# A graph layer's matrix product: batches taken in pairs, adjacency steps reordered, and spare matrix work while the degrees are computed

## What is computed

```python
# x: (8, 2048, 128)   adj: (2048, 2048)   W: (128, 128), all float32
h      = relu(layernorm(x))              # over the last axis
A      = relu((adj + adj.T) / 2)
D      = A.sum(1);  d = D ** -0.5
L      = eye - d[:, None] * A * d[None, :]
out    = x + relu(einsum('nm,bmo->bno', L, einsum('bnf,fo->bno', h, W)))
```

## Time and profile before

| | us |
|---|---|
| median of 3 timed executions (448.17 to 450.79) | 448.46 |
| the profiled execution's own time | 449.94 |
| its span, first to last instruction | 448.00 |
| busy: TensorE / weight loads | 398.3 / 208.6 |
| busy: DVE / ACT / POOL | 186.3 / 118.2 / 177.9 |
| mean granted TensorE clock, share of full | 0.954 |

### The profile page before, as it was taken

How to read it: one execution, slowest core, us unless ns; L and a number is a source line. 1 busy time by engine, 2 the same in 40 slices (tenths; PEclk the granted TensorE clock), 3 DMA queues, 4 the chain that set the end, 5 groups by cost and what they waited for, 6 DMA issues and landing times.

```text
span 448.0 us, 5765 instructions
## 1 busy us (share of the span) xinstructions
PE 398.3 (89%) x2179; PEld 208.6 (47%) x2179; DVE 186.3 (42%) x507; ACT 118.2 (26%) x247; POOL 177.9 (40%) x287
## 2 busy tenths in 40 slices
PE   3628672999399999999999999999999999999994
PEld 3628560444145444544454445554444444444442
DVE  3686756968368664764577012111111111111111
ACT  1464766543234433342344011000000000000000
POOL 0198900599965874877185001221211121111111
PEclk9888695899889999999999999999999999999998
DMA  8999970432104200230032003331111111111101
GB/s 280 356 359 384 382 193 23 118 104 85 47 1 119 72 0 1 76 113 1 1 94 72 23 1 94 95 94 48 47 48 47 48 47 48 47 49 47 47 25 47
DMA packets 59307, 42.38 MB, mean 95 GB/s; under 512 B 1808, under 2 KB 51088, under 8 KB 59280
## 3 DMA queue, kind: packets, MB, share of 16 engines
q1 hardware_dynamic: 59280, 42.02, 30.2%
HBM read 33.62 MB, written 8.39 MB: 94 GB/s over the span
## 4 chain that ended last, share of the span: by engine, by line
issue 41%; PE 26%; POOL 17%; SPq 5%; DVE 4%; ACT 4%; DMA 2%; POOLq 0%; ACTq 0%
PE ps L553 7%; PE ps L554 7%; PE ps L555 7%; POOL sums L275 6%; POOL hbuf L257 3%; SPq L179 3%; DMA S<-in_adj_dram 2%; ACT S L307 2%; POOL lnt L241 2%; SPq L193 2%; PE ps L514 2%; PE ps L528 2%; POOL dsv L266 2%; POOL xn L257 1%; DVE S L383 1%
## 5 line engine op out<-in xcount | busy, mean ns | idle before, releaser
L554 PE MATMUL ps<-S,hbuf 128*128 128x512 f16 x512 | 196.1, 383 | 0.0
L553 PE MATMUL ps<-S,hbuf 128*128 128x512 f16 x496 | 188.8, 381 | 7.1 <-DVE S L398 7.1
L555 PE MATMUL ps<-S,hbuf 128*128 128x512 f16 x496 | 188.7, 381 | 0.0
L275 POOL TENSOR_TENSOR sums<-res,sums 128x512 f32<-128x512 f32 x32 | 42.6, 1335 | 194.8 <-DVE res L411 192.9
L553 PEld LDWEIGHTS ps<-S,hbuf 128*128 128x128 f16 x496 | 48.7, 98 | 62.8 <-DVE S L398 7.6
L333 ACT ACTIVATE g<-ps 128x512 f16<-128x512 f32 x32 | 19.1, 597 | 221.1 <-PE ps L555 185.0
L554 PEld LDWEIGHTS ps<-S,hbuf 128*128 128x128 f16 x512 | 50.5, 99 | 57.6 <-issue 1.9
L555 PEld LDWEIGHTS ps<-S,hbuf 128*128 128x128 f16 x496 | 48.7, 98 | 59.0 <-issue 0.8
L403 DVE SCALAR_TENSOR_TENSOR g<-ps,g 128x512 f16<-128x512 f32 x32 | 21.9, 685 | 112.7 <-ACT g L333 112.6
L411 DVE SCALAR_TENSOR_TENSOR res<-ps,dsv 128x512 f32<-128x512 f32 x32 | 22.1, 692 | 88.2 <-PE ps L569 88.2
L327 ACT ACTIVATE S<-S,dneg 128x512 f16<-128x512 f32 x62 | 43.7, 716 | 37.4 <-DVE S L398 35.4
(11 more groups left out here) (67 smaller groups left out, 263.2 us busy)
## 6 DMA issues: line engine op xcount, KB each, us to landing
S<-in_adj_dram SPq DMA_DIRECT2D x16, 1024.0 KB, 11.0
hbuf<-in_x_dram SPq DMA_DIRECT2D x32, 256.0 KB, 4.5
sums<-in_x_dram SPq DMA_DIRECT2D x32, 256.0 KB, 2.7
out_dram<-sums SPq DMA_DIRECT2D x32, 256.0 KB, 2.3
res<-in_L_gnn_W_dram SPq DMA_DIRECT2D x1, 64.0 KB, 1.8
```

The costliest lines, as they stand in the source:

```text
L275: nc.gpsimd.tensor_tensor(sums[:, e % SUMS, :], res[:, e % 2, :], sums[:, e % SUMS, :], ALU.add).then_inc(sum_ready, 1)
L553: nc.tensor.matmul(acc, hbuf[:, u, 0, cols], l_hi(t), start=(mt == 0), stop=False)
L554: nc.tensor.matmul(acc, hbuf[:, u, 0, cols], l_lo(t), start=False, stop=False)
L555: last = nc.tensor.matmul(acc, hbuf[:, u, 1, cols], l_hi(t), start=False, stop=(mt == T - 1))
```

## The change

- **Pairs.** The batches go in four quarters of two. A unit is now two node tiles of two batches (the same 128 by 512 values, loaded by two DMAs of 128 KB). A quarter has eight units and four stages, a stage 16 mt of 2 x 3 matmuls. The total is the same 1,536. The 64 pieces of L are now cut and used during the first four of sixteen stages.
- **Whole steps.** All four groups of a step are turned first, then the mirrors of the step before. The step order puts (2,2) behind (2,3), so that (3,3) has no mirror beside it. DVE takes the mirrors k = 1 and 3.
- **x later.** Four units of x are loaded between the squares, twelve behind the last one. Units 4 and 5 have their statistics in the last adjacency step, and units 6 and 7 in the first step of the main loop. DVE's low halves of h come one adjacency step later than ACT's high ones.
- **Spare work.** `keep_busy` issues seven matmuls of 512 columns into a PSUM bank whose contents nobody reads: once when the last square has been added up, and once behind the turn of the maxima.
- **Degrees.** The small instructions are reordered, two of them ahead of the turned maximum and `take_diag(0)` behind it.
- **Lead and W.** `LEAD` is 6. `multiply_w` comes at mt 3 and 5 of the next stage (`W_AT`).

```diff
-DVE_MIRRORS = (3,)
+DVE_MIRRORS = (1, 3)
-LEAD = 2
+LEAD = 6
+PAIR = 2
+IDLE_TURNS = 7
+W_AT = (3, 5)
...
-    steps = [(i, j) for j in range(G) for i in range(j + 1)]
+    steps = [(0, 0), (0, 1), (1, 1), (0, 2), (1, 2), (0, 3), (1, 3), (2, 3), (2, 2), (3, 3)]
...
-    x_step = [0, 0, 1, 1, 2, 2, 3, 3, 4, 4, 9, 9, 9, 9, 9, 9]
-    stat_slot = [s + 1 - FRONT for s in x_step[:10]] + [0, 0, 2, 2, 4, 4]
-    h_slot = [max(0, u - H_LEAD) if u >= H_EARLY else -1 for u in range(T)]
-    h_slot += [12 + 3 * k for k in range(T)]
-    stat_slot += [h_slot[T + k - k % LN_BATCH] - 5 + k % LN_BATCH for k in range(T)]
+    x_step = [0, 0, 1, 2, 9, 9, 9, 9]
+    stat_slot = [-9,-9,-8,-7,-1, -1, 0, 0]
+    h_slot = [-7, -6, -5, -5, 0, 2, 4, 6]
+    h_slot += [16 + 6 * k for k in range(UNITS)] + [68 + 6 * k for k in range(2 * UNITS)]
+    stat_slot += [h_slot[UNITS + k - k % LN_BATCH] - 8 + k % LN_BATCH for k in range(3 * UNITS)]
...
-                for u in h_at.get(s - FRONT, []):
+                for u in h_at.get(s - 1 - FRONT, []):
                     split_h_lo(u)
...
                 for k in range(GRP):
                     turn_adj(s, k)
-                    for p in mirrors_at[s]:
-                        if k == 0:
-                            pe.wait_ge(s_ready, GRP * (p + 1))
+                for p in mirrors_at[s]:
+                    pe.wait_ge(s_ready, GRP * (p + 1))
+                    for k in range(GRP):
                         turn_mirror(p, k)
+            def keep_busy(bank):
+                for i in range(IDLE_TURNS):
+                    nc.tensor.matmul(ps[:, bank, :], hbuf[:, 0, 0, 0:P], hbuf[:, 0, 0, :], start=True, stop=True)
+            pe.wait_ge(a_added, GRP * len(steps))
+            pe.wait_ge(h_hi_ready, 1)
+            keep_busy(0)
             pe.wait_ge(max_ready, 1)
             nc.tensor.transpose(ps[:, 4, 0:P], gmax[:, 0:1].to_broadcast([P, P]), ident[:]).then_inc(max_turned, 1)
+            keep_busy(5)
...
+            for s in range(STAGES - 1):
+                for mt in range(T):
+                    if s < G:
+                        pe.wait_ge(l_lo_ready, s * T + mt + 1)
+                    if s % G == 0 and mt % PAIR == 0:
+                        pe.wait_ge(h_lo_ready, s // G * UNITS + mt // PAIR + 1)
+                    products(s, mt, range(PAIR))
+                    if s and mt in W_AT:
+                        multiply_w(PAIR * (s - 1) + W_AT.index(mt))
```

More of the change, by code:

```diff
@@ L28 @@
 SUMS = 3
-H_EARLY = 1
-H_LEAD = 3
 def gnn_layer(nc, x, adj, w, out):
@@ L129, in gnn_layer @@
         w_in = sem("w_in")
-        x_in = [sem(f"x_in{u}") for u in range(T)]
+        x_in = [sem(f"x_in{u}") for u in range(2 * UNITS)]
         x2_in = [sem(f"x2_in{s}") for s in range(4)]
@@ L200, in _, with reload_x @@
                     load_adj(j, i)
-                for u in range(T):
+                for u in range(UNITS):
                     if x_step[u] == s:
                         load_x(u)
+            for u in range(UNITS, 2 * UNITS):
+                load_x(u)
             for e in range(SUMS):
                 load_sums(e)
-            for k in range(T):
+            def reload_x(k):
                 sp.wait_ge(h_hi_ready, k + 1)
@@ L210, in _ @@
                 if k >= 4:
-                    sp.wait_ge(x2_in[k % 4], 16 * (k // 4))
-                load_x(T + k)
+                    sp.wait_ge(x2_in[k % 4], 16 * PAIR * (k // 4))
+                load_x(2 * UNITS + k)
+            for k in range(UNITS):
+                reload_x(k)
             for e in range(TILES):
+                for k in range(UNITS, 2 * UNITS):
+                    if h_slot[k] // T == e / PAIR:
+                        reload_x(k)
                 store_sums(e)
@@ L276, in add_x @@
                                         ALU.add).then_inc(sum_ready, 1)
-            for u in range(0, T, LN_BATCH):
+            for u in range(0, UNITS, LN_BATCH):
                 normalise(u)
@@ L282, in _ @@
                 scale_rows(s)
-            for tau in range(STEPS):
+            for tau in range(T * STAGES):
                 for u in stat_at.get(tau - 1, []):
-                    if u > T and u % LN_BATCH == LN_BATCH - 1:
+                    if u > UNITS and u % LN_BATCH == LN_BATCH - 1:
                         normalise(u - LN_BATCH + 1)
                 s = tau // T
-                if s and 1 <= tau % T <= GRP:
-                    add_x(GRP * (s - 1) + tau % T - 1)
-                    if tau % T == GRP:
+                if s and tau % T in W_AT:
+                    add_x(PAIR * (s - 1) + W_AT.index(tau % T))
+                    if tau % T == W_AT[-1] and s + 1 < STAGES:
                         scale_rows(s + 1)
[L292 to L295, removed]
+            for b in range(PAIR):
+                add_x(TILES - PAIR + b)
         @block.scalar
@@ L348, in _ @@
                 split_l_hi(t)
-            for tau in range(STEPS):
+            for tau in range(T * STAGES):
                 s = tau // T
-                if s and tau % T < GRP:
-                    split_g_hi(GRP * (s - 1) + tau % T)
+                if s and tau % T < PAIR:
+                    split_g_hi(PAIR * (s - 1) + tau % T)
                 if tau + LEAD < STEPS:
@@ L356, in _ @@
                     split_h_hi(u)
-            for e in range(GRP * (G - 1), TILES):
-                split_g_hi(e)
+            for b in range(PAIR):
+                split_g_hi(TILES - PAIR + b)
         @block.vector
@@ L497, in _ @@
                     statistics(u)
-            for e in range(GRP * (G - 1), TILES):
-                split_g_lo(e)
-                take_product(e)
+            for b in range(PAIR):
+                split_g_lo(TILES - PAIR + b)
+                take_product(TILES - PAIR + b)
         @block.tensor
@@ L570, in multiply_w @@
                 last.then_inc(prod_done, 1)
[L572 to L598, removed]
-                        if s == G and b < 2 and mt % 6 == 5:
-                            multiply_w(GRP * (G - 1) + 2 * b + mt // 6)
-                        if (s > G or b == 3) and mt == 5:
-                            multiply_w(GRP * s + b - 1)
-                        if s == G and b == 2 and mt in (5, 11):
-                            multiply_w(GRP * s + mt // 6)
+            for s in range(STAGES - 1):
[7 more added lines that the diff above has]
+                        multiply_w(PAIR * (s - 1) + W_AT.index(mt))
@@ L605, in _ @@
+            for b in range(PAIR):
+                for mt in range(T):
+                    products(STAGES - 1, mt, [b])
+                    if b == 0 and mt in W_AT:
+                        multiply_w(TILES - 2 * PAIR + W_AT.index(mt))
+                    if b == 1 and mt == W_AT[-1]:
+                        multiply_w(TILES - PAIR)
             multiply_w(TILES - 1)
```

100 lines of the change are left out of this document (50 added, 50 removed).

## The result

The changed kernel takes 432.88 us (median of 4 executions, 432.64 to 433.00) against 449.57 for the kernel before (4 executions). The ratio is 0.9629, 95% interval 0.9592 to 0.9666. The profiled execution took 432.93 us, its span is 431.1 and the mean granted clock 0.982. The forecast was 430.8, and 430.4 for the span.

The account below looks back on a forecast made before the run. TensorE was taken as the bound, busy nearly nine tenths of the span. Start 64.8 + matmuls 331.6 + `multiply_w` 20.7 + last result 7.3 + hole 4.0 + low clock 2.0 = 430.4 span; median 430.8, 80% range 422 to 441.

Parts of the forecast that it names:

- Squares earlier, turns in a row: Adjacency phase: squares land 5.4 us earlier, the mirror's wait goes, last turn at 55.5, additions end at 58.3.
- Degrees: From degree sum to first product: 4.35 us as before, the reordering worth zero; first product at 64.8.
- The clock at the start: Before and at the first products: clock stays high, so the 3.1 us of low clock go.
- The hole: Stage 0, piece 11 of L: TensorE waits 3.4 us behind h unit 6, then 2.0 us of low clock.
- the place in the queue: Stage 0 on DVE: the diagonal and piece 11 stand behind h unit 6, so piece 11 comes at 82.5.
- the term of 4.0: Stage 0: hole of 3.4 us plus 0.6 of small waits, given as between 1.3 and 5.1.
- Small waits: Stage 0: an estimated 0.6 us at piece 15 and for `multiply_w(1)`.
- Later stages: all at nothing: Stages behind stage 0: DVE's 67.6 of 88.3 us fits while POOL waits stay short, so no cost.
- No hole from stage 1 on: Sign to look for in TensorE's timeline: no hole from stage 1 on, nor at the start of stage 4.
- No hole: Rival, stage 0: POOL is quick and the lead of six covers unit 6; 422 to 427, chance 0.22.
- Turns slow: Rival, adjacency phase: low clock, five groups of turns and mirrors end 8.6 us later; 439, or 435; chance 0.12.
- Runs short through all four stages: Rival, stages cutting L: DVE waits for POOL and needs 97.6 of 88.3 us; 438, up to 441; chance 0.16.

Follow-up runs that it names:

- alternate: The changed kernel with turns and mirrors alternating group by group again, step order and all else kept: 436.05 us, ratio 0.9700.
- no_spare: The changed kernel without the fourteen spare matmuls (`IDLE_TURNS = 0`), nothing else changed: 433.04 us, ratio 0.9629.
- lag: x45_mid with the second quarter's h four steps later and its statistics where they were: 428.66 us, ratio 0.9532.
- h_late: The changed kernel with low halves of h units 6 and 7 two steps later, in steps 6 and 8 of the main loop: 432.77 us, ratio 0.9625.
- x45_mid: The changed kernel with x units 4 and 5 loaded behind step 4 of the squares, statistics of units 4 to 7 earlier: 430.72 us, ratio 0.9578.
- lag_only: The changed kernel with the second quarter's h four steps later, its statistics where they were: 431.36 us, ratio 0.9595.

## Why the prediction was right, point by point

- **Direction and size.** 430.8 forecast, 432.88 measured, inside 422 to 441. On the span 430.4 against 431.1. Term by term the start was 0.6 us earlier than forecast, the hole 0.1 longer, the low clock behind it 0.6 cheaper and the small holes 1.9 dearer: that the span came out within 0.7 is in part luck, since a miss of 1.2 one way made up for part of the 1.9 the other way. Two thirds of the miss of 2.1 us in the median come from the step from the profiled execution to the median: I took off 1.48 us because three executions of the kernel before had their median below its profiled one. The next executions were near 450 and the difference vanished.
- **Squares earlier, turns in a row.** (2,3) at 46.6, turned at 46.50. Last turn 55.5, measured 55.77. Additions end 58.3, measured 58.29. Degree sum 60.4, measured 60.31. alternate shows the turn order's part, 3.2 us.
- **Degrees.** 4.35 us to the first product was held unchanged, and 3.85 was measured. "Zero" for the new order was wrong by 0.5: from the turned maxima's start to `dneg` it is 1.37 us (60.96 to 62.33) and was 1.84 (72.63 to 74.47).
- **The clock at the start.** It stayed high, as I took it, and the spare work is the cause (no_spare). But the sum treated its 3.1 us as a gain of the whole. In this kernel it is worth nothing: no_spare takes the same time. And "stays high" was close: in lag the clock fell ahead of the first spare group.
- **The hole.** Forecast 3.4 us at piece 11 behind unit 6 on DVE; measured 3.5 there, released as said. The cause named first, the place in the queue, did not carry: h_late moved it and gained nothing. What carries is the second part of that step, POOL beside DVE's splits (x45_mid). The low clock behind it cost 1.4, not 2.0. The bounds given for the term of 4.0 (1.3 to 5.1) are those of the 3.4 alone, without the 0.6 of small waits.
- **Small waits.** 0.6 was the term, 2.5 was measured (0.9 of it in stage 0). "Later stages: all at nothing" is the step that failed. I compared DVE's work (67.6 of 88.3 us) with TensorE's and left out that DVE waits in order for POOL with results queued behind. lag_only gives the price, 1.5 us. "No hole from stage 1 on" was wrong for the same reason.
- **Rivals.** "No hole" at 422 to 427 was not reached even by lag, since units 4 and 5 cost a later start. "Turns slow" did not happen: all groups took 1.9 us. The Trainium skill, page "TensorE: Matmul & The Clock Gate", section "Part 4: PE-mode transpose", says that the high clock does not come for transposes. For the float32 turns of this kernel the trace speaks against it again: the clock was 1.00 in the window 54 to 56, where TensorE did nothing but turns. "Runs short through all four stages" happened at about a fifth of its price: 1.5 us in stages 1 to 3, where that rival added 7.3 to the forecast.

## What to carry to other kernels

While an engine is fed by slower ones, the holes and slow stretches in its timeline are one debt and can't be added: before pricing one of them, ask when the feeder would have been ready, and take the gain only up to that. A late start counts in full where it holds up the feeder too (alternate, 2.8 us at both places) and not where it gives the feeder time (x45_mid, start 2.8 later, piece 16 3.0 earlier). A variant that removes the debt first (here lag) shows what the other edits are worth. And when work is moved ahead in one engine's queue, look at what runs beside it: in h_late work that came early on DVE made POOL's come 2.0 us late.

## What the runs showed of the hardware that I had not expected

- POOL's L254, a product of 8 values a partition, took 0.34 us at its place in the changed kernel with DVE idle (0.20 in the adjacency phase) and 2.19 beside a run of DVE's splits and diagonals in h_late. Eight blocks of 128 by 128 took 3.46 us beside DVE's additions of squares and 7.25 and 8.74 beside its splits.
- With fourteen spare matmuls in two groups of seven, 1.7 us each and 0.9 us apart, the clock stayed at 1.00 up to the first product (changed kernel). Without them it fell to 0.50 (no_spare). In lag, with them, it fell and rose again from 0.50 to 1.00 ahead of the first product.
